# The causal mask of the row maxima, moved from TensorE products into VectorE's maximum; the first image pair normalised and convolved on its own, ahead of the others

## What is computed

```python
def reference(x, ...):
    x = x + _L0_conv_ref(_gn(x), offset_w, offset_b, weight, bias)   # offsets by a conv, bilinear samples
    t = _to_tokens(x)                                                 # 8 x 1024 tokens x 64
    t = t + _L1_attn_ref(_ln_t(t), w_q, w_k, w_v, w_o)                # causal, 16 heads, rotary q and k
    t = t + _L1_ffn_ref(_ln_t(t), sigma, phi, M_u, M_phi_plus, M_phi_minus, log_weights, gumbel)
    return _from_tokens(t, x)

def _gn(v, G=32, eps=1e-05):                  # two channels of an image are a group
    g = v.reshape(B_, G, C_ // G, H_, W_)
    m = jnp.mean(g, axis=(2, 3, 4), keepdims=True); s = jnp.var(g, axis=(2, 3, 4), keepdims=True)
    return ((g - m) / jnp.sqrt(s + eps)).reshape(v.shape)

# inside the attention
att = jnp.einsum('bqhd,bkhd->bhqk', q, k) / jnp.sqrt(E)
att = jnp.where(causal, att, -jnp.inf)
att = jax.nn.softmax(att, axis=-1)
```

## Time and profile before

| | |
|---|---|
| time, median of 3 runs (lowest, highest) | 2934.59 us (2934.13, 2935.37) |
| the profiled execution: its own time, its span | 2933.56 us, 2931.8 us |
| front, span 0 to about 202 us | POOL issues gathers for two thirds of it |
| attention, about 202 to 2280 us | PE busy 99% in the loop, DVE 81% |
| spectral, to the end | PE busy 96% |
| busy over the span | PE 94%, DVE 75%, POOL 59%, ACT 45% |

### The profile page before, as it was taken

How to read it: one execution, slowest core, us unless ns; L and a number is a source line. 1 busy time by engine, 2 the same in 40 slices (tenths; PEclk the granted TensorE clock), 3 DMA queues, 4 the chain that set the end, 5 groups by cost and what they waited for, 6 DMA issues and landing times. The chain is left out here.

```text
span 2931.8 us, 60696 instructions
## 1 busy us (share of the span) xinstructions
PE 2741.8 (94%) x18761; PEld 1789.2 (61%) x18761; DVE 2185.6 (75%) x3909; ACT 1330.1 (45%) x1788; POOL 1740.8 (59%) x1831
## 2 busy tenths in 40 slices
PE   3639999999999999999999999999998899999998
PEld 1335655655655655656655655655655788888887
DVE  3448788788788788788888888888886675767676
ACT  1103444444444444444444444444443465656565
POOL 3746777777777777777777777777776670000000
PEclk8659999999999999999999999999999899999999
DMA  5542222222222222222222212244443553444343
GB/s 151 145 112 59 64 63 62 64 63 58 68 63 58 68 63 58 64 67 58 65 67 58 65 54 69 65 64 60 64 65 55 161 168 116 147 130 146 116 154 105
DMA packets 159644, 249.21 MB, mean 85 GB/s; under 512 B 71662, under 2 KB 93502, under 8 KB 159582
## 3 DMA queue, kind: packets, MB, share of 16 engines
q1 hardware_dynamic: 125902, 155.61, 18.8%
q0 software_dynamic: 33680, 92.71, 13.1%
HBM read 230.65 MB, written 17.04 MB: 84 GB/s over the span
## 5 line engine op out<-in xcount | busy, mean ns | idle before, releaser
L1083 ACT ACTIVATE attention_probs<-attention_pss 128x1024 f32<-128x1024 f32 x576 | 590.1, 1024 | 310.7 <-PE attention_pss L920 298.4
L1286 POOL DMA_INDIRECT attention_gat<-table,attention_idx x585 | 558.5, 955 | 200.0 <-issue 121.3
L920 PE MATMUL attention_pss<-attention_kq 64*128 64x512 f32 (+3 forms) x3072 | 651.8, 483 | 0.0
L1149 DVE TENSOR_REDUCE attention_mx_half<-attention_pss 128x2 f32<-128x1024 f32 (+3 forms) x520 | 513.2, 1020 | 98.5 <-PE attention_pss L920 98.5
L1022 PE MATMUL attention_psY<-attention_probs,attention_xt 128*64 128x512 f32 (+3 forms) x3120 | 574.1, 496 | 0.2 <-issue 0.2
L1642 DVE SCALAR_TENSOR_TENSOR spectral_eo<-spectral_psE,kept_sig,spectral_eo 64x512 fp32r<-64x512 f32 x512 | 384.0, 750 | 170.1 <-ACT spectral_eo L1617 163.9
L1243 POOL TENSOR_TENSOR attention_kq<-attention_tA,attention_tB 128x512 f32<-128x512 f32 x260 | 416.1, 1611 | 111.0 <-DVE attention_tB L1159 101.7
L1535 PE MATMUL spectral_psE<-spectral_tz,spectral_up 128*128 128x512 f32 (+1 forms) x2304 | 462.1, 358 | 5.8 <-DVE spectral_up L1633 5.8
L1617 ACT ACTIVATE spectral_eo<-spectral_psE,kept_sig 64x512 fp32r<-64x512 f32 x512 | 350.2, 684 | 243.9 <-PE spectral_psE L1535 238.9
L920 PE MATMUL attention_pss<-attention_rows_m,attention_ones 64*128 64x512 f32 (+2 forms) x1536 | 458.8, 530 | 0.0
L1535 PEld LDWEIGHTS spectral_psE<-spectral_tz,spectral_up 128*128 128x128 f32 x2304 | 386.5, 189 | 78.2 <-issue 6.2
(11 more groups left out here) (192 smaller groups left out, 3199.0 us busy)
## 6 DMA issues: line engine op xcount, KB each, us to landing
spectral_tz<-phis SPq DMA_DIRECT2D x128, 320.5 KB, 4.6
spectral_tz<-phis SPq DMA_DIRECT2D x128, 320.0 KB, 4.2
attention_xb<-xn SPq DMA_DIRECT2D x132, 256.0 KB, 3.8
attention_gat<-table,attention_idx POOLq DMA_INDIRECT x585
table<-front_pixT SPq DMA_DIRECT2D x32, 288.0 KB
attention_wt<-in_w SPq DMA_DIRECT2D x66, 128.0 KB, 3.6
attention_xt<-xt SPq DMA_DIRECT2D x18, 128.0 KB, 2.1
attention_xs<-in_x SPq DMA_DIRECT2D x65, 32.0 KB
```

What stands on the lines that cost most here:

```text
L920: ins = pe.matmul(out(n), left(rows), right(rows), **flags)
L1083: act.activation(probs[:, u[1], :, :].rearrange("p n q -> p (n q)"), pss[:, slot, :], ACT.Exp, scale=float(E) ** -0.5).then_inc(s_act, 1)
L1149: ins = dve.tensor_reduce(mx[:, :, i] if i < 4 else mx_half[:, :, i - 4, k0 // 4], scores, AX.X, ALU.max)
L1286: pool.indirect_dma_start(gat[:, n, :, :].rearrange("p q c -> p (q c)"), None, d.table.rearrange("r q c -> r (q c)"), bass.IndirectOffsetO ...
```

## The change

It does two things.

1. **Attention.** The `mask_b` products go, with their tile and its cast. VectorE holds a tile `later` of 128 x 512 (zero, and -1e30 in the last 128 columns where the key is later). For a diagonal block, the one `tensor_reduce` over both heads becomes one `tensor_tensor_reduce` for each head: it adds the last columns of `later` to the scores, writes the sum back to the PSUM slot and gives the maximum as its accumulator. The blocks off the diagonal keep `tensor_reduce`. The wait for a filled slot in VectorE's units is now `wait_apart`, a wait with a semaphore increment of its own ahead of the instruction.
2. **Front.** SP loads the first pair, `pair_avg`, the identity and the offset weights first, then the other pairs, then the small vectors. Moments and the two averages run for pair 0 alone, then for pairs 1 to 3. The filter weights are made after `pad(0)`. TensorE transposes the pixels of pair 0 between the first taps of its convolution, and does the averages of the other pairs at taps 5 and 8. ScalarE follows (`pixels(0)` ahead of both `offsets`).

The diff, cut to its core:

```diff
-                for g in range(G):
-                    sp.dma_start(m.X[:, g, :], d.x[2 * g:2 * g + 2]...).then_inc(s_x, 16)
-                sp.dma_start(pair_avg[:, :], d.pair_avg).then_inc(s_const, 16)
+                sp.dma_start(m.X[:, 0, :], d.x[0:2].rearrange("b c h w -> (b c) (h w)")).then_inc(s_x0, 16)
+                sp.dma_start(pair_avg[:, :], d.pair_avg).then_inc(s_avgw, 16)
+                sp.dma_start(m.ident[:, :], d.ident).then_inc(s_ident, 16)
                 for h in range(2):
...
+                for g in range(1, G):
+                    sp.dma_start(m.X[:, g, :], d.x[2 * g:2 * g + 2]...).then_inc(s_x, 16)
+                sp.dma_start(lw[:, :], d.logw.partition_broadcast(P)).then_inc(s_small, 16)
+                sp.dma_start(gum[:, :], d.gumbel.partition_broadcast(P)).then_inc(s_small, 16)
+                sp.dma_start(sig_in[:, :], d.sigma.partition_broadcast(P)).then_inc(s_sig, 16)
@@ vector, front
+                dve.wait_ge(s_x0, 16)
+                moments(0, 1, 0)
                 pad(0)
+                each = Chain(dve, s_weights)
+                dve.wait_ge(s_small, 32)
+                each(dve.tensor_tensor(lw[:, :], lw[:, :], gum[:, :], ALU.add))
...
+                dve.wait_ge(s_x, 16 * (G - 1))
+                moments(1, G, 1)
                 pad(1)
+                dve.wait_ge(s_const, 32)
@@ tensor, front
                     for tap in range(K2):
+                        if g == 0 and tap in (0, 2, 4):
+                            pixels(0, range(4 * (tap // 2), min(4 * (tap // 2) + 4, NCH)))
+                        if g == 0 and tap == 5:
+                            averages(1, 1, G)
+                        if g == 0 and tap == 8:
+                            squares(1, 1, G)
@@ scalar, front
+                act.wait_ge(s_sq, 2)
+                act.activation(dev[:, 0:1], gn_var[:, 0:1], ACT.Sqrt).then_inc(s_std, 1)
                 act.wait_ge(s_ex, 1)
                 act.activation(soft[:, :], lw[:, :], ACT.Exp).then_inc(s_soft, 1)
+                pixels(0)
+                act.wait_ge(s_sq, 4)
+                act.activation(dev[:, 1:G], gn_var[:, 1:G], ACT.Sqrt).then_inc(s_std, 1)
+                act.wait_ge(s_offw, 96)
+                offsets(0)
+                offsets(1)
+                pixels(1)
@@ tensor, attention, unit "max"
                             first += nk * P
-                            if k0 + nk == i + 1:
-
-                                for a in range(2):
-                                    ins = both(lambda n: out[:, n * HB + first - P:n * HB + first],
-                                               lambda rows: mask_b[rows, 1 + a, :], lambda rows: mask_b[rows, 3 + a, :],
-                                               start=False, stop=True, skip_group_check=True)
@@ vector, attention
-                    dve.wait_ge(s_full, n + 1)
+                    wait_apart(dve, s_full, n + 1, s_apart)
...
-                            ins = dve.tensor_reduce(mx[:, :, i] if i < 4 else mx_half[:, :, i - 4, k0 // 4], scores, AX.X, ALU.max)
+                            top = mx[:, :, i] if i < 4 else mx_half[:, :, i - 4, k0 // 4]
+                            if k0 + nk == i + 1:
+                                for n in range(2):
+                                    ins = dve.tensor_tensor_reduce(scores[:, n, :], scores[:, n, :], later[:, HB - nk * P:HB], 1.0,
+                                                                   LOWEST, ALU.add, ALU.max, top[:, n:n + 1])
+                            else:
+                                ins = dve.tensor_reduce(top, scores, AX.X, ALU.max)
```

142 lines of the change are left out of this document (64 added, 78 removed).

## The result

The changed kernel takes **2950.34 us** (median of 5, 2950.07 to 2951.69) against 2934.59 us (5 runs, 2934.13 to 2938.47) for the kernel before: ratio 1.0052, 95% interval 1.0038 to 1.0067. It is slower by half a per cent, where I had predicted faster by 0.6%. Its profiled execution has a span of 2948.4 us, against 2931.8.

The account below looks back on a forecast made before the run. It took a ScalarE and VectorE chain to bound each head pair's tail, PE the rest, and GpSimd's gather start the front. 2933.6 - 4.5 (loop) + 1.6 (pass ahead) - 14 (front) gave 2917 us, range 2896 to 2955.

Parts of the forecast that it names:

- PE's other 25 us of a head pair are PE's alone: Attention loop outside the tail: PE waits for no other engine during 25 us of each head pair.
- dear reads: Rival on VectorE's accumulator reads: up to 0.27 us each instead of 0.07, 2963 us in all; chance 0.18.
- What bounds the tail: From `dR` to `row`: a ScalarE and VectorE chain as long as PE's work, about 0.05 us to spare.
- Part 1: Masks off PE: 1.04 us less per head pair, of which 0.65 ahead of `dR` counts and the tail's nothing.
- Part 2: Maxima on VectorE: its part of the tail takes 2.50 us instead of 1.92, 0.58 longer per head pair.
- So I cost them at nothing: VectorE ahead of the tail: ten more reads and five more main instructions cost nothing, given some 6 us to spare.
- an idle PE of about 0.6 + 0.39 us: Expected sign ahead of `row` if the forecast was right: PE stands idle that long, waiting for `merge`.
- Pass ahead of the loop: Eight diagonal blocks on VectorE before the attention loop, PE waiting: 0.20 us more each, +1.6 us.
- Part 3: Front, first image pair taken ahead: the start of the gathers comes sooner, -14 us, with ends -15.8 and -11.
- Free reads: Rival on VectorE's accumulator reads: 0.01 to 0.02 us each, tail 0.33 shorter than forecast, 2896 us; chance 0.12.
- The front did not keep its time: Rival on the front: table or index set hardly sooner, gain 3 us instead of 14, 2928 us; chance 0.09.
- PE as the bound of the whole: Rival on the loop: VectorE keeps up in the tail, all 67 us come, 2855 us; within the rest's 0.03.

Follow-up runs that it names:

- run without masks: Kernel before with the front part, TensorE's mask products left out and VectorE's maxima as before: 2887.15 us, ratio 0.9833 to the kernel before.
- second execution: The kernel before run once more without any edit: 2936.45 us, one run.
- waits alone: Kernel before with the front part and VectorE's separate counting waits, masks and maxima unchanged: 2936.26 us, ratio 0.9996 to the kernel before.
- tail_k_by_pe: Kernel before with the front part; VectorE adds the mask in a, c, d, i, TensorE keeps mask products of j, b, k: 2897.66 us, ratio 0.9864.
- moved_gather: tail_k_by_pe with GpSimd's third group of gathers issued right after the second: 2911.43 us, ratio 0.9913 to the kernel before.

## Why the prediction was wrong

The sign was wrong. The step that failed first is the sentence "PE's other 25 us of a head pair are PE's alone", with the price of nothing for VectorE's extra work there: PE waits at `dT` and at `out` 1, and ahead of the tail it gained 0.455 us and not 0.65, 12.5 us over the loop. The second is a term that the sum did not have, the clock, 8.4 us. That the measured time lies inside the range is luck: its upper part was there for dear reads, and a read costs 0.03 to 0.04 us.

*What bounds the tail: right.* The chain through ScalarE and VectorE ends the tail: the run without masks has the tail to 0.01 us where it was. PE ends the rest only outside `dT` and `out` 1.

*Part 1, 0.65 us ahead of `dR`: too high.* The masks off PE bring 0.57 (run without masks). The products do cost 0.12 to 0.13 each, those of d 0.18, but the 0.12 of k fills a wait of `dT`: the step of `out` 0 and `dT` grows by what k shrinks. I had added up PE's work over a stretch in which I took PE to wait for nobody.

*Part 2, the tail: the size of the new instructions was right, the rest was not.* Mains and reads with the gap to `merge` were to take 2.42 and take 2.44, but by errors that cancel: the six mains are 0.09 dearer, the five reads between them 0.16 cheaper (0.04 each against 0.07), and the last read to `merge` takes 0.18 against 0.11. The wait was to add 0.08 and adds 0.15. And `xn`, which I had not looked at, got 0.08 longer, where GpSimd's instruction now lies over it. Together 0.75 in place of 0.58.

*"So I cost them at nothing": wrong, by 0.11 us in each head pair.* Ahead of the tail VectorE has 6 us to spare in sum, but k is read and `out` 1 waits for its slot. I had named k as the next to hold PE if the reads were dear. It holds PE with cheap reads: VectorE's work on k is 1.41 us from its start to the last read's end where it was 1.23. With the mask products kept on PE it costs `out` 1 0.23 us, in the changed kernel 0.11, as the wait at `dT` hides the rest.

*What no step had: the clock.* The tail's two gaps make PE stand still around `row`, and at five passages the clock falls to 0.50 and PE loses 1.7 us each. I had the gaps in the list of what would be seen ("an idle PE of about 0.6 + 0.39 us") and gave them no price beyond their length.

The loop was to change by -4.5 us (a head pair of 31.4) and changed by +25.7 (31.87). The 30 us between them are: 12.5 from the part ahead of the tail (0.65 - 0.455, 64 times), 4.5 from the wait, 5 from `xn`, 1 from the mains and reads, 8.4 from the clock. That adds up to 31, the pieces being rounded. The last stretch adds 2.6 us that the second execution shows to be within its own variation.

*Pass ahead of the loop*: forecast +1.6; from the first product of the attention to the first `row` it went from 27.2 to 29.2 us, but the second execution of the kernel before has 28.4, so the size can't be told. The granted clock is at 1.00 for 10.2 us of that stretch in the first execution and for 6.8 in the other two, and at 0.50 in the rest of it.

*Part 3, the front: right in its places.* Convolution or transposes at 12.9 (14.3 forecast), first store 21.7 (20.8), gathers 36.9 (near 35), the first product of the attention 13.8 us sooner (14). The 2 us that I allowed for the moments were 2.9. By the times the front alone gives 8.3.

*The rivals.* Dear reads, the one on the slower side, did not happen: a read costs 0.04, far below the 0.115 from which it was to decide. The kernel is slower all the same, by several smaller prices together, none of which alone turns the sign. Free reads, at 0.01 to 0.02, came a little nearer to the truth on the reads than my 0.07. The front did not keep its time. PE as the bound of the whole is excluded by the run without masks: of 67 us on PE it brings the loop 36. That a follower starts ahead of the recorded end of the one before, which I had held against the dear reads, holds for the new instruction too: at j the second main starts at 1020.99, and the record of the first ends at 1020.77 + 0.30 = 1021.07.

## What to carry to other kernels

When work moves from a busy engine to one with slack, ask at each hand-over which of the two is late there; a sum of slack over the whole period hides nothing at a slot that the busy engine waits for. Against the loop of the kernel with the front part alone, the same instruction brought 25 us where VectorE's tail was left as it was, and cost 25 where it was used everywhere. And in this kernel new gaps on TensorE had a price beyond their length where they fell together with one that was there already: 1.7 us at each of five places of seven.

## What the runs showed of the hardware that I had not expected

- TensorE's granted clock fell from 1.00 to 0.50 for 3.4 us at a time at places with three gaps of 0.48, 0.51 and 0.8 us close together, not always but at five of seven like places of the changed kernel; with the first gap at 0.03 or gone (0 to 0.5 us ahead of `row`, 0.8 ahead of `rope` 0) it fell at none.
- Writing out the accumulator of the add-and-maximum instruction is recorded as 0.14 us, with a start equal to that of the next instruction, and cost 0.03 to 0.04 us in spacing.
- A satisfied wait as an instruction of its own on VectorE cost 0.11 us on the path ahead of a `tensor_reduce` (waits alone) and 0.15 ahead of the new instruction (changed kernel).
- `xn`, a VectorE instruction of 64 elements that takes 0.31 us, took 0.50 in `tail_k_by_pe` while GpSimd issued a gather, and the copy of 63 (0.19 us) took 0.56 in `moved_gather` under a mask instruction; the same copy keeps its 0.19 us when it starts 0.08 to 0.43 us into a descriptor instruction.
